# Accumulator adds of an expert layer, split into halves and issued ahead of the gate product

## The reference

```python
x = x + _layernorm(_L0_attn_ref(_layernorm(x), w_lhs, w_rhs))
x = x + _layernorm(_L0_ffn_ref(_layernorm(x), ...))

# _L0_ffn_ref
shared = jax.nn.silu(xf @ shared_w1.T) * (xf @ shared_w2.T) @ shared_w3.T
scores = jax.nn.sigmoid(xf @ router_w.T)
_, top_idx = jax.lax.top_k(scores + expert_bias, TOP_K)
mask = jax.nn.one_hot(top_idx, N_EXPERTS, dtype=xf.dtype).sum(axis=-2)
gates = scores * mask
h12 = jnp.einsum('td,ehd->teh', xf, w12)
h1, h2 = jnp.split(h12, 2, axis=-1)
h = jax.nn.silu(h1) * h2 * gates[:, :, None]
routed = jnp.einsum('teh,edh->td', h, w3)
return (shared + routed).reshape(b, s, d)
```

## Time and profile before

| | |
|---|---|
| median of the runs | 2945.62 us |
| lowest run | 2938.82 us |
| profiled execution, its own time | 2939.12 us |
| span of the profiled execution, slowest core (4) | 2937.6 us |
| spans of the 8 cores | 2927.2 to 2937.6 us |
| mean granted TensorE clock, core 4 | 0.963 |

### The profile page before, as it was taken

How to read it: one execution, slowest core, us unless ns; L and a number is a source line. 1 busy time by engine, 2 the same in 40 slices (tenths; PEclk the granted TensorE clock), 3 DMA queues, 4 the chain that set the end, 5 groups by cost and what they waited for, 6 DMA issues and landing times.

```text
span 2937.6 us, 47617 instructions; the slowest of 8 cores (2927.2 to 2937.6 us)
## 1 busy us (share of the span) xinstructions
PE 2449.9 (83%) x17186; PEld 1664.2 (57%) x17186; DVE 1103.8 (38%) x2263; ACT 439.5 (15%) x1048; POOL 243.0 (8%) x462
## 2 busy tenths in 40 slices
PE   0387887679999989999999867999999999999991
PEld 0123333356766666666666645676666666666661
DVE  3504336342222444343444433222244444444444
ACT  2022222101111111111111111111111111111111
POOL 0000010101110111001110110111001110111000
PEclk9999888899999999999999989999999999999996
DMA  5301135605433553245423562553245523553203
GB/s 150 97 1 45 42 60 138 105 2 87 66 52 57 87 87 56 40 79 87 72 40 63 87 111 90 87 83 52 50 77 87 83 36 56 87 87 54 35 1 115
DMA packets 80730, 204.76 MB, mean 70 GB/s; under 512 B 10537, under 2 KB 10858, under 8 KB 80490
## 3 DMA queue, kind: packets, MB, share of 16 engines
q0 software_dynamic: 65952, 151.11, 32.6%
q1 hardware_dynamic: 14546, 50.61, 5.3%
HBM read 335.91 MB, written 16.84 MB: 120 GB/s over the span
## 4 chain that ended last, share of the span: by engine, by line
PE 71%; DVE 17%; DMA 4%; issue 4%; ACT 2%; DVEq 1%; SPq 0%; POOL 0%; ACTq 0%; POOLq 0%
PE h1p L828 20%; PE outp L755 20%; PE h1p L838 20%; DVE acc L774 7%; PE stp L454 4%; DMA x2r<-x2s 2%; PE aop L483 2%; PE aop L486 1%; PE gatesp L813 1%; ACT s1t L850 1%; DMA xr<-x 1%; DVE Gt L862 1%; DVE t2t L858 1%; DVE Gt L867 1%; DVEq L1016 1%
## 5 line engine op out<-in xcount | busy, mean ns | idle before, releaser
L850 ACT ACTIVATE s1t<-h1p 128x256 f32<-128x256 f32 x768 | 295.0, 384 | 1973.7 <-PE h1p L838 1972.2
L858 DVE TENSOR_TENSOR t2t<-h1p,gb 128x256 f32<-128x256 f32 x512 | 217.5, 425 | 834.1 <-ACT s1t L850 793.7
L755 PE MATMUL outp<-sBw,Gt 128*128 128x512 bf16 x1536 | 394.3, 380 | 93.2 <-DVE acc L774 90.5
L755 PE MATMUL outp<-sAw,Gt 128*128 128x512 bf16 x1536 | 397.9, 382 | 81.6 <-DVE acc L774 73.6
L828 PE MATMUL h1p<-n2fm,sAw 128*128 128x256 bf16 x3072 | 404.2, 275 | 34.4 <-DVE Gt L867 34.4
L838 PE MATMUL h1p<-n2fm,sAw 128*128 128x256 bf16 x3072 | 401.9, 274 | 0.0
L828 PE MATMUL h1p<-n2fm,sBw 128*128 128x256 bf16 x3072 | 401.9, 274 | 0.0
L838 PE MATMUL h1p<-n2fm,sBw 128*128 128x256 bf16 x3072 | 400.4, 274 | 0.0
L828 PEld LDWEIGHTS h1p<-n2fm,sAw 128*128 128x128 bf16 x3072 | 299.0, 99 | 154.2 <-issue 48.7
L828 PEld LDWEIGHTS h1p<-n2fm,sBw 128*128 128x128 bf16 x3072 | 299.4, 98 | 121.6 <-issue 11.5
L838 PEld LDWEIGHTS h1p<-n2fm,sAw 128*128 128x128 bf16 x3072 | 302.5, 98 | 36.9
(11 more groups left out here) (103 smaller groups left out, 1061.6 us busy)
## 6 DMA issues: line engine op xcount, KB each, us to landing
sAw<-w12t POOLq DMA_DIRECT2D x64, 512.0 KB, 16.7
sBw<-w12t POOLq DMA_DIRECT2D x64, 512.0 KB, 15.8
xr<-x SPq DMA_DIRECT2D x48, 512.0 KB, 4.3
sAw<-w3t POOLq DMA_DIRECT2D x64, 256.0 KB, 30.3
sBw<-w3t POOLq DMA_DIRECT2D x64, 256.0 KB, 29.8
x2s<-x2t SPq DMA_DIRECT2D x16, 512.0 KB, 5.1
sAw<-w1t POOLq DMA_DIRECT2D x32, 256.0 KB, 13.7
sAw<-w2t POOLq DMA_DIRECT2D x32, 256.0 KB, 14.6
```

Source lines behind the costliest of these rows:

```text
L755: inst = e.matmul(outp[tt][:, half * 512:(half + 1) * 512], Gt[jj_ % 4][:, tt * P:(tt + 1) * P], w3t_[j_][:, half * 512:(half + 1) * 512], ...
L850: E("scalar", lambda e, jj=jj, v=evv: e.activation(s1t[jj % 3][:], h1p[jj % 3][:, 0:TBLK], ACT.Silu).then_inc(S["s_ev"], 1))
L858: E("vector", lambda e, jj=jj, tb=tb: e.tensor_mul(t2t[jj % 2][:], h1p[jj % 3][:, TBLK:2 * TBLK], gate_b[tb % 2][:]), drain=True)
```

## The change

The two operations that move outp to acc become four, one for each half of 512 columns. They are no longer written at once but put into a list, `acc_q`, which is emptied between the Silu and the gate product of the same step. The second layer is now written ahead of the Silu; since these stand on different engines, TensorE's order stays. Each half's semaphore value is kept in `acc_free`, and each of the four matmuls that begin new sums waits for the value of its own half.

```diff
         def emit_s2_fix(p):
             (jj_, j_, w3t_, first_acc_wait, _unused_v, s2v, accs) = p
-            if first_acc_wait:
-                W("tensor", S["s_acc"], cur(S["s_acc"]))
             for tt in range(TT_PER_TB):
                 for half in range(2):
+                    if first_acc_wait:
+                        W("tensor", S["s_acc"], acc_free.get((tt, half), 0))
...
             if accs is not None:
                 ci_, tb_ = accs
-                W("vector", S["s_s2"], s2v)
-                for tt in range(TT_PER_TB):
-                    ai = tb_ * TT_PER_TB + tt
-                    av = inc(S["s_acc"])
-                    if ci_ % NCHUNK_P == 0:
-                        E("vector", lambda e, tt=tt, ai=ai, v=av: e.tensor_copy(
-                            acc[ai][:], outp[tt][:]).then_inc(S["s_acc"], 1), drain=True)
-                    else:
-                        E("vector", lambda e, tt=tt, ai=ai, v=av: e.tensor_add(
-                            acc[ai][:], acc[ai][:], outp[tt][:]).then_inc(S["s_acc"], 1), drain=True)
-                    if ci_ % NCHUNK_P == NCHUNK_P - 1:
-                        acc_tile_ready[(ci_ // NCHUNK_P, ai)] = av
-                        emit_stats_pre(ci_ // NCHUNK_P, ai)
+
+                def emit_accs(ci_=ci_, tb_=tb_, s2v=s2v):
+                    W("vector", S["s_s2"], s2v)
+                    for tt in range(TT_PER_TB):
+                        ai = tb_ * TT_PER_TB + tt
+                        for half in range(2):
+                            av = inc(S["s_acc"])
+                            acc_free[(tt, half)] = av
+                            hs = slice(half * 512, (half + 1) * 512)
+                            if ci_ % NCHUNK_P == 0:
+                                E("vector", lambda e, tt=tt, ai=ai, hs=hs, v=av: e.tensor_copy(
+                                    acc[ai][:, hs], outp[tt][:, hs]).then_inc(S["s_acc"], 1), drain=True)
+                            else:
+                                E("vector", lambda e, tt=tt, ai=ai, hs=hs, v=av: e.tensor_add(
+                                    acc[ai][:, hs], acc[ai][:, hs], outp[tt][:, hs]).then_inc(S["s_acc"], 1), drain=True)
+                        if ci_ % NCHUNK_P == NCHUNK_P - 1:
+                            acc_tile_ready[(ci_ // NCHUNK_P, ai)] = av
+                            emit_stats_pre(ci_ // NCHUNK_P, ai)
+                acc_q.append(emit_accs)
...
                     s1v = cur(S["s_s1"])
+                    ev2 = inc(S["s_ev2"])
+                    s2v = inc(S["s_s2"], TT_PER_TB)
+                    first_acc_wait = (j == 0) and not (ci == 0 and tb == 0)
+                    accs = (ci, tb) if j == NCD - 1 else None
+                    this = (jj, j, w3_t, first_acc_wait, None, s2v, accs)
+                    s2_pending.append((this, ev2))
+                    if len(s2_pending) > S2_DEPTH:
+                        p, pev2 = s2_pending.pop(0)
+                        emit_s2_fix(p)
                     W("scalar", S["s_s1"], s1v)
                     evv = inc(S["s_ev"])
                     E("scalar", lambda e, jj=jj, v=evv: e.activation(
                         s1t[jj % 3][:], h1p[jj % 3][:, 0:TBLK],
                         ACT.Silu).then_inc(S["s_ev"], 1))
+                    while acc_q:
+                        acc_q.pop(0)()
                     W("vector", S["s_ev"], evv)
```

More of the change, by code:

```diff
@@ L742, in emit_pass @@
         s2_pending = []
+        acc_q = []
         def emit_s2_fix(p):
             (jj_, j_, w3t_, first_acc_wait, _unused_v, s2v, accs) = p
-            if first_acc_wait:
-                W("tensor", S["s_acc"], cur(S["s_acc"]))
             for tt in range(TT_PER_TB):
                 for half in range(2):
+                    if first_acc_wait:
+                        W("tensor", S["s_acc"], acc_free.get((tt, half), 0))
                     lastj = j_ == NCD - 1
@@ L860, in emit_pass @@
                             gate_b[tb % 2][:]), drain=True)
-                        ev2 = inc(S["s_ev2"])
                         E("vector", lambda e, jj=jj, v=ev2: e.tensor_mul(
@@ L869, in emit_pass @@
                             h1p[jj % 3][:, TBLK:2 * TBLK]).then_inc(S["s_ev2"], 1), drain=True)
[L870 to L877, removed]
                     jj += 1
@@ L882, in emit_pass @@
             emit_s2_fix(p)
+        while acc_q:
+            acc_q.pop(0)()
     acc_tile_ready = {}
+    acc_free = {}
     stats_pre_done = set()
```

## The result

The changed kernel takes 2849.49 us (median of 8 runs, 2846.48 to 2852.74); of the ten runs of the kernel before seven took 2938.82 to 2945.62. The ratio is 0.9687, with a 95% interval of 0.9676 to 0.9698: 92 us, 3.1% faster. Forecast were 84 us and 2855.

A forecast was written before the change was run, and what follows sets the result against it. TensorE and its waits for DVE's acc adds (189.8 us delay) were taken to bound the kernel. Delay after 106.8 saves 83.0, less 3.9 gives 79.1, plus 5 for the clock: 2939.1 - 84 = 2855 us, range 2836 to 2886.

The forecast's parts named there:

- points 1 to 3: Block boundary, from S, the last second-layer group's start: adds start at 1.13, pieces take 0.69 us, next first layer at 4.53.
- point 4: Last chunk of a pass, reduce between the tiles: next first layer at S + 5.90, where it was 6.92.
- point 5: Third step's Gt, now behind the pieces, ends near S + 5.4; cover 1.7 us, 0.5 in last chunk; cost nothing.
- point 7: TensorE's clock falls less after long waits, as the longest idle drops below 2 us; 5 us gained.
- the working's 79.1: Gain at all boundaries without the clock: 83.0 us less 3.9 for router, phase E and pass ends.
- Group release: Rival: all four matmuls wait for the last piece, first layer at S + 5.17; 2920 us; chance 0.08.
- the split of idle that this rival feared: Rival: broken-up idle makes TensorE's clock fall at most boundaries, 1.6 us each; 3004 us; chance 0.05.
- A costly piece: Rival: each half add on DVE costs far more than 0.69, up to 1.22 us; 3062 us; chance 0.03.
- a late Gt: Rival: DVE finishes Gt 0.65 us late at each boundary, TensorE waits three steps on; 2915 us; chance 0.06.
- point 6: First block beside the router, phase E and both passes' ends: no gain there, together 3.9 us lost.

The follow-up runs named there:

- order alone: Against the changed kernel: adds still ahead of the gate product, but whole (1024 elements) and with one wait for both; 2865.88, 2868.6 and 2869.2 us, ratio 0.9743.
- Halves alone: Against the changed kernel: same four half adds with a wait each, but in the old place behind the gate product; 2931.6 us, ratio 0.9959.
- the two doses of reduces: Changed kernel plus one or two unread DVE reduces behind the four adds, except in a pass's last chunk; one 2852.27 and 2853.48 us, two 2931.9.
- One wait: Changed kernel's four half adds in their new place, but all four matmuls wait for the last half; 2916.8 us, ratio 0.9912.

## Why the prediction was right

**The boundary (points 1 to 3).** All of it came out: the start at S + 1.13, pieces of 0.687 for 0.69, the third and fourth matmul at 3.52 and 4.30 for 3.53 and 4.31, the next first layer at 4.52 in the expert block and 4.54 in the shared one for 4.53. The piece's size was read off a line through three sizes, and the start off the one place in the trace where the add already waited for TensorE. Both were there before the change ran.

**What carries it.** The prediction gave the gain as one sum. The runs divide it: 75 us from the order alone and 12 from the halves alone, the slow clock's part included. The working would have told so: without Gt in front the adds start 0.88 or 0.31 earlier, while halves release TensorE by 0.65 sooner and lengthen DVE's work by 0.50, a net of 0.15. At 64 expert and 29 shared boundaries the order alone saves 65 us by that.

**The last chunk (point 4)** came out: the first layer at 1633.24 follows S at 1627.35 by 5.89, for 5.90:

```profile
1627.35 1.03 PE L756 MATMUL outp<-sBw,Gt 128*128 128x512 bf16 x4
...
1631.41 1.47 DVE L780 TENSOR_TENSOR acc<-acc,outp 128x512 f32<-128x512 f32 x2
...
1632.24 0.38 PE L756 MATMUL outp<-sBw,Gt 128*128 128x512 bf16 x1 [1.69 <-DVE acc L780]
...
1633.24 1.03 PE L835 MATMUL h1p<-n2fm,sBw 128*128 128x256 bf16 x8
```

**Gt's cover (point 5)** was put at nothing with 1.7 us to spare; Gt ended at S + 5.38 for 5.4, and the two doses of reduces bracket the cover between 1.31 and 2.62; the wait of 0.98 behind the second puts it at 1.64.

**The clock (point 7)** came out in its sign, but not by the reason given. I counted 5 us. Read over all eight cores, the granted clock fell at 43 ordinary boundaries before (five or six on each core) and at 4 after, none on five cores; at 1.6 us each that is 7.8 us for the mean core. Between the two slowest cores, 4 before with five falls and 6 after with two, it is 4.8, the 5 that I counted. The half that I gave to the last chunks was too little: there it mostly stays at full too. The reason given was that the longest idle comes below 2 us. **Halves alone** refutes it: at 24 boundaries outside the last chunks four idles of 0.34 to 0.42 each are followed by the slow clock, while **One wait** with one idle of 1.53 to 1.90 keeps 1.00 there on all cores. So that the clock would gain was in part luck. The changed kernel idles twice and 0.72 us in all at most expert boundaries, where **Halves alone** idles three or four times and the kernel before once for 1.92 to 2.20 at most of them; which of these keeps its clock no run separates. The Trainium skill's rule on psum-queue depth-cycling, by which repeated short idles bring the slow clock, is not borne out in the changed kernel: two idles of 0.32 and 0.40 at each boundary keep it at 1.00 in both windows above. In **Halves alone**, with four idles, the trace agrees with it at those 24 boundaries.

**The sum.** The two profiled executions differ by 86.9 us, the means of their eight core spans (2932.5 and 2844.7) by 87.8. For the mean core the working's 79.1 and 7.8 for the clock make 86.9. The further 5 us up to the 92 of the ratio lie within the spread of single runs (2938.8 to 2945.6 before, 2846.5 to 2852.7 after) and aren't assigned.

**The rivals.** Group release did not happen by itself; forced by one wait it costs 67 us and gives 2916.8, beside the 2920 that its sum had. The clock fell less, not more, though the split of idle that this rival feared is not harmless, as **Halves alone** shows. A costly piece and a late Gt did not come.

**The router and phase E (point 6).** No run tried them alone, but the traces have them, as means over the eight cores and with the slow clock there included. From the Silu of step 8 to that of step 24, where the working loses 1.0 us beside the router, the changed kernel is 2.2 slower. The four blocks beside phase E, from step 384 to 416, gain 4.4, where the working has 1.3 for their three waits. The two ends lose 0.5 and 0.4, for 0.5 each. The attention ahead of it all, which the change does not touch, took 1.8 longer. Misses of this size, 1.2, 3.1 and 1.8, partly cancel; that the total is so close owes something to this.

## What to carry to other kernels

When the first engine waits for a PSUM tile to be read out, measure from the end of the last write to the end of the last reading piece, and first look at what stands ahead of that reading in its engine's queue: here a gate product that nobody needed for another five microseconds. Cutting the reading into pieces pays only as far as it lets the next writer start within its own due time; beyond that each further piece adds its fixed cost to the wait (here 0.15 us of busy time and 0.09 between two operations), and two pieces with a wait each beat four. Breaking an idle into more pieces can also bring the slow clock where one longer idle did not, so count the falls on all cores. If another engine is idle, let it read half.

## What the runs showed of the hardware

- DVE and ScalarE read two tiles of PSUM at the same time at their own speeds: 1.22 us for the add and 1.02 for the copy of 128 x 1024, side by side, with TensorE writing other banks.
- In the kernel before the clock fell after an idle of 2.20 us at 1101 and 1388 but not at 1197.99, where the idle was as long; on all eight cores it fell at these same two boundaries. In the changed kernel it fell at 4 boundaries over eight cores, each with an idle of 1.68 us and one of 0.40. What sets the difference between equal idles was not tried.
- With its read-out in four pieces behind the gate product (**Halves alone**) TensorE idles four times 0.34 to 0.42 us at some boundaries, and the clock fell at 24 of these over eight cores, outside the last chunks; with one idle of 1.53 to 1.90 in the same place (**One wait**) it fell at none.
- A satisfied wait ahead of a matmul costs nothing measurable in 2692 cases.
